# The output products of a quantised feed-forward layer as one pipeline of 16 parts, with work moved between ScalarE, VectorE and GpSimd

## Time and profile before

| what | us |
|---|---|
| median of 3 runs | 165.79 (165.48 to 166.21) |
| the profiled execution, its own time | 165.92 |
| its span, first to last instruction | 163.8 |
| end of the hidden products and their reduction (L941) | 129.6 |
| stage of the change, L941 to the last output's data | 129.6 to 163.1 |
| outputs issued from SP | 8 of 256 KB, 2.1 to landing |

### The profile page before, as it was taken

The page is one execution under the profiler, slowest core; times in us unless marked ns, Lnnn a source line. Parts: engine busy times, 40 slices in busy tenths (PEclk is TensorE's granted clock), DMA queues, the critical chain, the costliest instruction groups (busy, mean ns, idle before and its releaser), DMA issues.

```text
span 163.8 us, 2952 instructions
## 1 busy us (share of the span) xinstructions
PE 154.5 (94%) x1126; PEld 112.5 (69%) x1129; DVE 126.1 (77%) x269; ACT 111.3 (68%) x179; POOL 40.4 (25%) x43
## 2 busy tenths in 40 slices
PE   7999999999999999999999789999999789999990
PEld 5898476787666888996658564444445468888880
DVE  0007879999588759446999879999877799999963
ACT  3265512979862556464489979998889399999900
POOL 8002210008600073000059600199000033320000
PEclk9999999999999999999999999999999999999999
DMA  5999999400000000000000000000000000003306
GB/s 148 264 318 399 403 355 394 139 4 2 4 0 0 0 4 0 0 0 4 0 2 0 0 4 0 0 0 0 4 0 0 0 0 4 0 0 128 133 0 256
DMA packets 6284, 12.16 MB, mean 74 GB/s; under 512 B 576, under 2 KB 3904, under 8 KB 6016
## 3 DMA queue, kind: packets, MB, share of 16 engines
q1 hardware_dynamic: 6272, 11.99, 21.4%
HBM read 9.89 MB, written 2.10 MB: 73 GB/s over the span
## 4 chain that ended last, share of the span: by engine, by line
PE 84%; DVE 8%; ACT 5%; issue 1%; DVEq 0%; POOL 0%; POOLq 0%
PE ps L1256 15%; PE ps L1042 9%; PE ps L1021 9%; PE ps L1231 8%; PE ps L1226 8%; PE ps L999 5%; PE ps L1033 4%; PE ps L1164 4%; PE ps L986 4%; PE ps L1178 3%; PE ps L1074 2%; PE ps L1173 2%; DVE sm L849 2%; DVE sm L932 1%; PE ps L1085 1%; ACT arena L634 1%
## 5 line engine op out<-in xcount | busy, mean ns | idle before, releaser
L1256 PE MATMUL ps<-woutq,arena 128*128 128x256 f16 x256 | 28.7, 273 | 1.3 <-ACT arena L634 0.7
L1256 PEld LDWEIGHTS ps<-woutq,arena 128*128 128x128 f16 x256 | 24.7, 98 | 5.3 <-ACT arena L634 1.5
L619 ACT ACTIVATE arena<-ps,colv,sm 128x512 f32<-128x512 f32 x32 | 23.9, 777 | 2.3 <-PE ps L1231 0.5
L953 DVE SCALAR_TENSOR_TENSOR arena<-scr,sm,arena 128x1024 f16<-128x1024 int16 x16 | 21.3, 1372 | 0.0
L932 DVE TENSOR_REDUCE sm<-arena 128x1 f32<-128x1024 f32 (+1 forms) x17 | 18.9, 1148 | 2.5 <-ACT arena L619 2.5
L1231 PE MATMUL ps<-arena,winq 128*128 128x512 bf16 x64 | 18.6, 379 | 0.1
L1226 PE MATMUL ps<-arena,winq 128*128 128x512 bf16 x61 | 17.9, 379 | 0.3 <-DVE arena L897 0.3
L634 ACT ACTIVATE arena<-arena,sm 128x1024 f16<-128x1024 f32 x15 | 16.4, 1134 | 0.0
L1042 PE MATMUL ps<-wvo,arena 128*128 128x256 f32 x64 | 15.9, 389 | 0.0
L986 PE MATMUL ps<-ones 128*128 128x256 bf16 x96 | 14.1, 303 | 1.0 <-POOL ones L375 1.0
L1021 PE MATMUL ps<-arena,wqk 128*128 128x512 f32 x32 | 14.4, 598 | 0.0
(11 more groups left out here) (201 smaller groups left out, 283.1 us busy)
## 6 DMA issues: line engine op xcount, KB each, us to landing
arena<-x_dram SPq DMA_DIRECT2D x4, 512.0 KB, 9.5
out_dram<-arena SPq DMA_DIRECT2D x8, 256.0 KB, 2.1
arena<-ctx_in_dram SPq DMA_DIRECT2D x4, 448.0 KB, 6.0
tabs<-tab_dram SPq DMA_DIRECT2D x1, 1264.5 KB, 14.1
arena<-winT_dram SPq DMA_DIRECT2D x1, 1024.0 KB, 15.6
arena<-turn_dram SPq DMA_DIRECT2D x1, 1024.0 KB, 11.7
arena<-wout_dram SPq DMA_DIRECT2D x1, 1024.0 KB, 12.4
arena<-wqT_dram SPq DMA_DIRECT2D x1, 256.0 KB, 7.8
```

The lines of the kernel that those rows point to most:

```text
L619: a.activation(H[:, f, 512 * c:512 * c + 512], bank("M1", n), ACT.Gelu, bias=colv[:, 6 + f:7 + f], scale=sc1[:, f:f + 1]).then_inc(S["h_re ...
L953: v.scalar_tensor_tensor(out=part, in0=scr16[:, n % 4, :], scalar=rf[:, f:f + 1], in1=piece(Hhi, n), op0=ALU.mult, op1=ALU.subtract).then_ ...
L1256: return t.matmul(o[k // 2][:, 256 * (k % 2):256 * (k % 2) + 256], part[:, t0:t0 + 128], woutq[:, f, :], start=start, stop=stop)
```

```diff
-        DVE_ROUNDS = (0, 1, 3, 7, 11)
-        POOL_ROUNDS = (5, 9, 13)
+        DVE_ROUNDS = (0, 1, 3, 7)
+        POOL_ROUNDS = (5, 8, 11, 14)
+
+        POOL_FINALS = (2, 3)
+
+        def finished(i):
+            by_pool = sum(k <= i for k in POOL_FINALS)
+            return (S["o_p"], by_pool) if i in POOL_FINALS else (S["o_ready"], i + 1 - by_pool)
...
-            for i in range(8):
-                sp.wait_ge(S["o_ready"], i + 1)
+            for i in (0, 1, 2, 4, 3, 5, 6, 7):
+                sp.wait_ge(*finished(i))
                 sp.dma_start(out[i], xs[:, 512 * i:512 * i + 512]).then_inc(S["out_done"], 16)
...
+            for n, i in enumerate(POOL_FINALS):
+                pool.wait_ge(S["oc_ready"], n + 1)
+                g.tensor_tensor(xs[:, 512 * i:512 * i + 512], scr[:, 0, 512 * n:512 * n + 512], xs[:, 512 * i:512 * i + 512], ALU.add)\
+                 .then_inc(S["o_p"], 1)
...
-            for n in range(16):
+            high(1)
+            for n in range(2, 16):
                 high(n)
-                if n < 15 and n + 1 not in DVE_ROUNDS + POOL_ROUNDS:
-                    rounded(n + 1)
+                if n not in DVE_ROUNDS + POOL_ROUNDS:
+                    rounded(n)
+            act.wait_ge(S["sc2_ready"], 1)
+            act.wait_ge(S["hq_ready"], 13)
+            for n, i in enumerate(POOL_FINALS):
+                filled(act, "M2", i)
+                a.mul(scr[:, 0, 512 * n:512 * n + 512], bank("M2", i), sc2).then_inc(S["oc_ready"], 1)
...
+            dve.wait_ge(S["hsc_ready"], 1)
+            for k in range(2):
+                v.tensor_scalar(piece(Hhi, 0)[:, 512 * k:512 * k + 512], piece(H, 0)[:, 512 * k:512 * k + 512], hrf[:, 0:1], None,
+                                ALU.mult).then_inc(S["hhi_d"], 1)
             rounded(0)
+            low(0)
+            rounded(1)
+            low(1)
...
-            for n in range(16):
-                if n + 1 in DVE_ROUNDS:
-                    rounded(n + 1)
+            for n in range(2, 16):
+                if n in DVE_ROUNDS:
+                    rounded(n)
                 low(n)
-                if 9 <= n < 13:
-                    final(n - 9)
+                if n in (10, 12):
+                    final(n // 2 - 5)
             for i in range(4, 8):
                 final(i)
...
+            high_products(0)
+            high_products(1)
+            for n in range(2, 15):
+                high_products(n)
+                low_products(n - 2)
+            low_products(13)
+            pe.wait_ge(S["hhi_ready"], 15)
+            pe.wait_ge(S["hq_ready"], 16)
+            o = outputs[1]
+            for k in range(8):
+                product(o, k, Hlo8[:, 2], 1, 6)
+                product(o, k, Hhi[:, 7], 1, 7)
+                last = product(o, k, Hlo8[:, 3], 1, 7, stop=(k % 2 == 1))
+                if k % 2:
+                    done(last)
```

More of the change, by code:

```diff
@@ L213, in build @@
                  "wom_ready wg_ready rf_ready yu_ready yhi_ready yq_ready h_ready hm_ready ha_ready hsc_ready "
-                 "yq_scale hhi_first hu_a hu_d hu_p hhi_ready hq_ready o_ready out_done ct_ready ones_ready pool_chain iv_a x2_p y_p yhi_d xt_a xt_d identb_ready").split()
+                 "yq_scale hhi_d oc_ready sc2_ready o_p hu_a hu_d hu_p hhi_ready hq_ready o_ready out_done ct_ready ones_ready pool_chain iv_a x2_p y_p yhi_d xt_a xt_d identb_ready").split()
         S = {n: sem(n) for n in names}
@@ L270, in build @@
             "HM2": lambda i: [(S["hsc_ready"], 1)],
-            "M2": lambda i: [(S["o_ready"], i + 1)],
+            "M2": lambda i: [],
         }
@@ L949, in low @@
                 f = n % 8
-                dve.wait_ge(S["hhi_ready"], n + 1)
+                dve.wait_ge(*(S["hhi_ready"], n) if n else (S["hhi_d"], 2))
                 dve.wait_ge(*rounded_by(n))
@@ L960, in final @@
                  .then_inc(S["o_ready"], 1)
+            dve.wait_ge(S["hsc_ready"], 1)
+            for k in range(2):
+                v.tensor_scalar(piece(Hhi, 0)[:, 512 * k:512 * k + 512], piece(H, 0)[:, 512 * k:512 * k + 512], hrf[:, 0:1], None,
+                                ALU.mult).then_inc(S["hhi_d"], 1)
             rounded(0)
+            low(0)
+            rounded(1)
+            low(1)
             link(v.tensor_scalar(sc2, hb, 1.0 / 127.0, None, ALU.mult))
-            link(v.tensor_scalar(sc2, sc2, wg, None, ALU.mult))
+            v.tensor_scalar(sc2, sc2, wg, None, ALU.mult).then_inc(S["sc2_ready"], 1)
+            dve.wait_ge(S["sc2_ready"], 1)
             dve.wait_ge(S["x2b_ready"], 1)
-            for n in range(16):
-                if n + 1 in DVE_ROUNDS:
-                    rounded(n + 1)
+            for n in range(2, 16):
+                if n in DVE_ROUNDS:
+                    rounded(n)
                 low(n)
-                if 9 <= n < 13:
-                    final(n - 9)
+                if n in (10, 12):
+                    final(n // 2 - 5)
             for i in range(4, 8):
@@ L1259, in _ @@
             pe.wait_ge(S["woutq_ready"], 1)
[L1260 to L1285, removed]
-                for k in range(8):
-                    product(o, k, Hhi[:, 7], c, 7)
-                    last = product(o, k, Hlo8[:, 3], c, 7, stop=(k % 2 == 1))
-                    if k % 2:
-                        done(last)
@@ new lines, in _, with high_products @@
+            outputs = [[take_bank(pe, "M2", 4 * c + k) for k in range(4)] for c in range(2)]
+            def high_products(n):
+                c, f = n // 8, n % 8
+                if n == 0:
+                    pe.wait_ge(S["hhi_d"], 1)
+                else:
+                    pe.wait_ge(S["hhi_ready"], n)
+                for k in range(8):
+                    if n == 0 and k == 4:
+                        pe.wait_ge(S["hhi_d"], 2)
+                    product(outputs[c], k, Hhi[:, f], c, f, start=(f == 0 and k % 2 == 0))
@@ new lines, in low_products @@
+            def low_products(n):
+                c, f = n // 8, n % 8
+                pe.wait_ge(S["hq_ready"], n + 1)
+                for k in range(8):
+                    last = product(outputs[c], k, (Hlo5 if f < 4 else Hlo8)[:, f % 4], c, f, stop=(n == 7 and k % 2 == 1))
+                    if n == 7 and k % 2:
+                        done(last)
+            high_products(0)
[3 more added lines that the diff above has]
+                low_products(n - 2)
```

## The result

The changed kernel takes 169.24 us (median of 4 runs, 168.93 to 169.95), the kernel before 165.63 in the same comparison: a ratio of 1.0214, 95% interval 1.0193 to 1.0234. It is slower by 2.1%. The prediction said slower, 167.0 and at most 168.5; the measured time lies 0.7 above its range.

A forecast was written before the change was run, and what follows sets the result against it. The prediction took the stage as bound by TensorE's products, VectorE hardly less loaded. Final sum 4 coming 0.49 later plus 0.68 for a fifth output made 1.17 on 165.92, 167.1, less 0.13 for the median: 167.0 us, range 165.2 to 168.5.

The forecast's parts named there:

- The head of the stage: Start of the output stage: high part 0 moves to VectorE, first product at 130.22, about 1.0 us of three gaps saved.
- The price of a GpSimd rounding: VectorE's queue: each GpSimd rounding costs VectorE about 0.79 us, or 0.43 behind a final sum.
- The mechanism of the sums: End of VectorE's queue: GpSimd's first sum makes low part 15 stand still and end 1.07 us later, at 158.18.
- the share of the outputs: Tail: five transfers instead of four follow final sum 4, which adds 0.68 us.
- the sign: Whole kernel: slower with chance 0.59, same 0.27, faster 0.14.
- the rounding that gains VectorE nothing: VectorE's queue: a rounding given to GpSimd costs VectorE no less than the 0.66 us pitch it takes over.
- the sum of VectorE's queue: VectorE up to low part 15: changes sum to about 0.1 us, ending at 157.2 without GpSimd's sums, as before.
- the four dependent waits: VectorE's queue: low parts 0, 1, 3, 7 wait for the rounding directly ahead, 0.12 us each, +0.48 in all.
- the first rival: Both GpSimd sums go ahead of a low part if VectorE is 0.15 or more late: 168.4 us, chance 0.15.
- the forecast's picture: End of VectorE's queue: first sum arrives within low part 14, only low part 15 is held up; 167.0 us, chance 0.52.
- a sum takes the next change: GpSimd's sum arriving during low part 14 runs when that has read, about 155.83 to 157.1, ahead of low part 15.
- a gap of 1.8: TensorE idles 1.8 us ahead of the last 24 products; a clock fall there would add time, left unpriced.

## Why the prediction was wrong

**Right.** The head of the stage: first product 0.67 behind the scales (forecast 0.66), high 0 in 0.49 with a pitch of 0.40, gaps of 0.14, 0.22 and 0.13 at H3, L2 and L3 where 0.2 each was said. The price of a GpSimd rounding: L2 2.02, L10 2.06, L11 1.70. Two roundings held up another operation than I had said: R8 let L6 go by and held up VectorE's own R7 (1.53 instead of 0.75), and R11 let L9 go by and held up L10, each at the same cost. The mechanism of the sums, the share of the outputs and the sign were right, and the rounding that gains VectorE nothing was confirmed in the kernel before as well.

**The step that failed.** It is the sum of VectorE's queue, in the term of the four dependent waits. I priced them at 0.12 each (0.48 in all) and gave 0 to 0.12 as bounds, so the price was its own upper bound. It came from small operations of the kernel before, where one follows its source 0.035 behind its end:

```profile
130.13 0.14 DVE L963 TENSOR_SCALAR sm<-sm 128x1 f32<-128x1 f32 x1
130.31 0.21 DVE L964 TENSOR_SCALAR sm<-sm 128x1 f32<-128x1 f32 x1
```

In the changed kernel a low behind its own rounding follows 0.11 behind its end; L2, behind a small operation that it waits for, follows 0.035 behind:

```profile
130.03 0.75 DVE L958 TENSOR_SCALAR scr<-arena,sm 128x1024 f32<-128x1024 f32 x1
130.89 1.28 DVE L965 SCALAR_TENSOR_TENSOR arena<-scr,sm,arena 128x1024 f16<-128x1024 int16 x1
...
134.34 0.21 DVE L983 TENSOR_SCALAR sm<-sm 128x1 f32<-128x1 f32 x1
134.58 2.02 DVE L965 SCALAR_TENSOR_TENSOR arena<-scr,sm,arena 128x1024 f16<-128x1024 int16 x1
```

The rounding ends at 130.78, the low starts at 130.89; with the pitch of 0.66 that is 0.20 lost each time, or about 0.8 for the four. They made VectorE 0.31 later than my times (L15 at 27.98 with the sums held back; forecast 27.67). Why the low starts later than the small operations do is open. That it waits for two things, its high part and its rounding, doesn't explain it alone: L2 waits for four and starts 0.035 behind.

**What it turned over.** I had S2 arrive 0.14 behind L14's start and wrote that the outcome changes if VectorE is 0.15 behind. S2 came 0.12 later than I had it (ScalarE's copy took 0.68, where I had 0.59), VectorE 0.31, and S2 stood 0.05 ahead of L14. So the first rival came true, with 0.15 of the chance: L15 at 30.02 where the forecast had 28.62 (158.18 less 129.56). Both single corrections bring the forecast's picture back: S2 0.2 later (L15 at 29.00) or VectorE without the dependent waits (28.19). That a sum takes the next change when it comes during a low was itself without a row: the rounding at 133.88 which I cited for it came during a rounding of VectorE (133.62 to 134.37) and let a whole low go by the earlier trace rows. The run with S2 a little later bears the rule out for a sum. A margin of 0.15 with an unknown of 0.5 beside it was no ground for 0.52 against 0.15; the two cases should have had about the same chance, and the range should have reached further above the second.

**What was named but not priced.** The rival's 168.4 had no fall of the clock. That is worth 0.5 in the medians (168.74 against 169.24), more than half of the 0.8 between the rival and the measurement, and 0.75 behind the scales in the profiled executions. The range ended at 168.5, at the rival's own time, with nothing for the clock, although the text said that a gap of 1.8 could bring it down; the gap in that rival is longer still.

**The five outputs.** Forecast 0.68; 0.81 in the profile, from the first issue behind final 4 to the end of the data. With the clock kept it is 4.4 (161.42 to 165.8) against 3.72, about the 0.68 of the forecast. So the fifth transfer was priced rightly, and the other 0.13 goes with the half clock: finals 5 and 6 come later behind final 4, and the data dips to 299 GB/s.

## What to carry to other kernels

An operation moved to GpSimd that reads SBUF is not free for VectorE where VectorE reads two inputs from SBUF, and here VectorE's roundings, with one input, were held up as well (1.53 instead of 0.75): count what it holds up in VectorE's queue (0.79 here for a rounding of 1.12, 1.0 for a sum of 1.27), and place it beside operations that read PSUM, where a rounding cost 0.43. Where a forecast hangs on which of two operations arrives first, and they are closer than the error of the sum, give both outcomes the same weight. Whoever puts an operation directly behind the one that it depends on should price the wait from a row of the same two operations, or bound it well on both sides, and outputs that are all issued at the end form a queue of their own: count them behind the last one that releases them.

## What the runs showed of the hardware that was not expected

Which change of VectorE's operation GpSimd gets is not settled by arrival alone. R8 and R11 of the changed kernel were issued at 139.96 and 145.18, 0.18 behind the start of a low (139.77 and 145.00), and each let the next low go by; both sums, in the changed kernel and in the one with S2 a little later, got the first change that came. In the kernel before, R5 let one go by and R9 did not the earlier trace rows. The roundings read one input and the sums two, but this was not tried apart, and it stays open. The rule of the Trainium skill that the prediction named ("SBUF — State Buffer", "Who interferes with whom": whoever issues first goes first) agrees with both sums and not with R8 and R11.

In the profiled executions the granted clock held through a gap of 1.98 and fell to half after one of 3.01; at half, 8 products took 1.64 of the window from 159 to 161, and at full, in the run with the clock kept, 16 took 1.61 of the same window.
